# Opening of a four-net modulated-convolution kernel: products on ones, an earlier first tap, scale tables and level steps in another order

## What is computed

```python
def _layer(x, style, w, b, mw, mb, typ):
    s = style @ mw.T + mb
    weight = SCALE * w * s[:, None, :, None]
    demod = lax.rsqrt(jnp.sum(weight * weight, axis=(2, 3)) + EPS)
    weight = weight * demod[:, :, None, None]
    ...
x = x + _L0_attn_ref(_L0_cond_ref(x, cond_512, L0_cond_weights, ...), L0_attn_Wqkv, L0_attn_Wo)
x = x + _L0_ffn_ref(_L0_cond2_ref(x, cond_512, ...), ...)
x = x + _L1_attn_ref(_L1_cond_ref(x, cond_512, ...), ...)
x = x + _L1_ffn_ref(_L1_cond2_ref(x, cond_512, ...), ...)
```

## Time and profile before

| what | value |
|---|---|
| median of 3 runs | 1014.01 us (1013.42 to 1014.83) |
| the profiled execution, its own time | 1012.35 us |
| its span, first to last instruction | 1010.6 us |
| mean granted TensorE clock over the span | 0.987 |
| TensorE busy | 957.1 us, 95% |
| VectorE busy | 556.2 us, 55% |
| GpSimd busy | 469.1 us, 46% |
| ScalarE busy | 232.3 us, 23% |

### The profile page before, as it was taken

The page is one execution under the profiler, slowest core; times in us unless marked ns, Lnnn a source line. Parts: engine busy times, 40 slices in busy tenths (PEclk is TensorE's granted clock), DMA queues, the critical chain, the costliest instruction groups (busy, mean ns, idle before and its releaser), DMA issues.

```text
span 1010.6 us, 15965 instructions
## 1 busy us (share of the span) xinstructions
PE 957.1 (95%) x6766; PEld 712.3 (70%) x6766; DVE 556.2 (55%) x951; ACT 232.3 (23%) x451; POOL 469.1 (46%) x425
## 2 busy tenths in 40 slices
PE   6899999999999999999999879989989999899997
PEld 2337887877887788887888658846857777446953
DVE  7866748567284753848458435243347969302423
ACT  4602122211122212022120210110052666500001
POOL 7934538485575846758376332301322645220300
PEclk9999999999999999999999989989999999999999
DMA  5782101111110111110113075393470000072002
GB/s 137 177 248 67 57 1 43 73 42 53 43 42 32 42 53 42 73 42 2 53 42 111 17 150 152 84 225 55 185 271 1 3 3 3 2 162 67 4 1 83
DMA packets 36287, 74.30 MB, mean 74 GB/s; under 512 B 13492, under 2 KB 22260, under 8 KB 33140
## 3 DMA queue, kind: packets, MB, share of 16 engines
q1 hardware_dynamic: 35880, 72.89, 25.9%
q10 hardware_dynamic: 336, 0.39, 0.1%
HBM read 66.26 MB, written 7.01 MB: 73 GB/s over the span
## 4 chain that ended last, share of the span: by engine, by line
PE 73%; DVE 11%; POOL 6%; ACT 4%; issue 3%; DMA 1%; SPq 0%; POOLq 0%; DVEq 0%; ACTq 0%
PE ps L1208 15%; PE ps L1146 14%; PE ps L1007 8%; PE ps L1462 5%; PE ps L1280 5%; PE ps L1160 4%; POOL w_lo L2354 3%; DVE arena L2010 3%; ACT acts L1507 2%; PE ps L1385 2%; DVE arena L2007 2%; PE ps L1285 1%; DVE h_lo L2019 1%; PE ps L1387 1%; PE ps L1386 1%
## 5 line engine op out<-in xcount | busy, mean ns | idle before, releaser
L2469 POOL TENSOR_TENSOR arena<-arena 128x512 f32<-128x512 f32 x80 | 103.6, 1295 | 122.7 <-DVE arena L2010 122.6
L1146 PE MATMUL ps<-xt_hi,w_hi 128*128 128x512 f32 x320 | 127.8, 399 | 5.5 <-POOL w_lo L2354 2.7
L1146 PE MATMUL ps<-xt_lo,w_hi 128*128 128x512 f32 x320 | 125.5, 392 | 0.0
L1146 PE MATMUL ps<-xt_hi,w_lo 128*128 128x512 f32 x320 | 125.2, 391 | 0.0
L1208 PE MATMUL ps<-h_hi,wo_hi 128*128 128x512 f32 x256 | 104.9, 410 | 11.9 <-DVE h_lo L2019 11.9
L2028 DVE TENSOR_TENSOR fresh<-ps,fresh 128x512 f32<-128x512 f32 x56 | 38.7, 691 | 133.9 <-PE ps L1208 133.8
L2010 DVE TENSOR_TENSOR arena<-ps,rope 64x512 f32<-64x512 f32 x160 | 110.2, 689 | 2.2
L1208 PE MATMUL ps<-h_lo,wo_hi 128*128 128x512 f32 x256 | 103.1, 403 | 0.0
L1208 PE MATMUL ps<-h_hi,wo_lo 128*128 128x512 f32 x256 | 102.4, 400 | 0.0
L2377 POOL TENSOR_TENSOR xt<-arena 128x512 f32<-128x512 f32 x24 | 30.5, 1270 | 136.9 <-DVE arena L1915 136.9
L1600 ACT ACTIVATE h_hi<-ps 128x512 fp32r<-128x512 f32 x64 | 33.1, 603 | 203.1 <-PE ps L1193 203.1
(11 more groups left out here) (325 smaller groups left out, 1882.8 us busy)
## 6 DMA issues: line engine op xcount, KB each, us to landing
acts<-in_w_o_dram SPq DMA_DIRECT2D x8, 1024.0 KB, 5.0
arena<-in_a_wo_dram SPq DMA_DIRECT2D x8, 1024.0 KB, 5.9
arena<-kernel_rows SPq DMA_DIRECT2D x11, 512.0 KB, 11.7
acts<-in_w_qkv_dram SPq DMA_DIRECT2D x3, 1792.0 KB, 7.0
acts<-in_w_qkv_dram SPq DMA_DIRECT2D x4, 1280.0 KB, 6.6
w_l<-kernel_rows SPq DMA_DIRECT2D x10, 512.0 KB, 11.8
arena<-level_rows SPq DMA_DIRECT2D x4, 1024.0 KB, 21.8
stream<-in_x_dram SPq DMA_DIRECT2D x4, 512.0 KB, 6.7
```

The source lines that it names most:

```text
L1146: last = pe.matmul(ps[:, bank, :], w[:, r, cols], x, start=(r == 0 and n == 0), stop=(r == R - 1 and n == 2))
L2469: pool.tensor_tensor(qk[:, chunk, half * HALF:(half + 1) * HALF], rot[:, k % 2, 0, :], rot[:, k % 2, 1, :], ALU.add).then_inc(s_rope, 1)
```

## The change

- TensorE gets 22 products of `ones` with itself (128 columns, into the sixth bank, where no one reads them): 8 ahead of the style products, 4 ahead of net 0's demodulation product, 10 behind it.
- The factors get a semaphore of their own, `s_factor`, and GpSimd's opening waits for that one (and for net 0's taps) alone. `s_setup` counts biases and identity.
- GpSimd makes the zeros of net 0's kernel ahead of net 1's upsampling taps.
- VectorE: `tile_scales` is split. `second_scales` (the tables that need no root) comes earlier, the rest behind the third stage's tiles. The styles of nets 1 to 3, the layer biases and the tap sums come later between the tiles.
- TensorE's level steps, and VectorE's, come later: the first behind net 1's first stage, not in front of it; `turn_levels` behind net 2's first stage.

```diff
-            sp.dma_start(factor[:, :, :], a["factor"]).then_inc(s_setup, 16)
+            sp.dma_start(factor[:, :, :], a["factor"]).then_inc(s_factor, 16)
...
-        N_SETUP = 16 * 3
+        N_SETUP = 16 * 2
...
+            def keep_clock(count):
+
+                for _ in range(count):
+                    pe.matmul(ps[:, COMPOSE - 1, 0:P], ones[:, :], ones[:, :], start=True, stop=True)
+
+            pe.wait_ge(s_const, 1)
+            keep_clock(8)
             pe.wait_ge(s_mod, 48)
...
+            keep_clock(4)
             pe.wait_ge(s_sq, 1)
             demod((0,), 4)
+            keep_clock(10)
...
             kernel_second(1)
+            kernel_first(1)
             level_step(0)
-            kernel_first(1)
+            kernel_third(2)
             level_step(1)
-            kernel_third(2)
+            kernel_second(2)
             level_step(2)
-            kernel_second(2)
+            kernel_first(2)
             turn_levels()
-            kernel_first(2)
             kernel_third(3)
...
+            def second_scales(ns):
+                ch.mark(dve.tensor_copy(in_scale[:, ns, :], s4[:, ns, 0, :]))
+                ch.mark(dve.scalar_tensor_tensor(mid_scale[:, ns, 1, :], s4[:, ns, 1, :], CONV_SCALE, s4[:, ns, 2, :],
+                                                 ALU.mult, ALU.mult))
+                if ns.start:
+                    ch.wait()
+
             def tile_scales(ns):
-                dve.tensor_copy(in_scale[:, ns, :], s4[:, ns, 0, :])
                 for layer in range(2):
                     last = dve.reciprocal(d4[:, ns, layer, :], d4[:, ns, layer, :])
-                dve.scalar_tensor_tensor(mid_scale[:, ns, 1, :], s4[:, ns, 1, :], CONV_SCALE, s4[:, ns, 2, :],
-                                         ALU.mult, ALU.mult)
...
             turn_taps(slice(0, 1))
+            second_scales(slice(0, 1))
             first_scales(slice(0, 1))
+            scaled_tiles(0, range(4))
             tile_scales(slice(0, 1))
             turn_taps(slice(1, 2))
-            scaled_tiles(0, range(4))
+            scaled_tiles(0, range(4, 6))
             styles(slice(1, NET), 7)
-            scaled_tiles(0, range(4, 6))
+            scaled_tiles(0, range(6, 8))
             turn_taps(slice(2, NET))
-            scaled_tiles(0, range(6, 8))
             first_scales(slice(1, NET))
             scaled_tiles(0, range(8, 13))
+            second_scales(slice(1, NET))
+            scaled_tiles(1, range(4))
             tile_scales(slice(1, NET))
-            scaled_tiles(1, range(4))
+            scaled_tiles(1, range(4, 8))
             layer_biases()
+            scaled_tiles(1, range(8, 11))
             tap_sums()
-            scaled_tiles(1, range(4, 8))
+            scaled_tiles(1, range(11, 13))
             level_step(0)
-            scaled_tiles(1, range(8, 13))
+            scaled_tiles(2, range(4))
             level_step(1)
...
-            pool.wait_ge(s_setup, N_SETUP)
+            pool.wait_ge(s_factor, 16)
             first_taps(slice(0, 1))
             upsampled(0, slice(0, 1))
             first_taps(slice(1, NET))
-            upsampled(1, slice(1, 2))
             kernel_zeros(0, 0)
             kernel_zeros(0, 2)
+            upsampled(1, slice(1, 2))
```

5 lines of the change are left out of this document (3 added, 2 removed).

## The result

| | before | changed |
|---|---|---|
| median of 20 runs each, on one chip | 1014.23 us (1012.74 to 1017.21) | **1019.65 us** (1014.42 to 1027.10) |
| ratio to before, 95% interval | | **1.0056** (1.0037 to 1.0074) |
| profiled execution, its span | 1012.35, 1010.6 | 1027.10, 1025.1 |
| mean granted clock of that execution | 0.987 | 0.977 |
| first convolution of the stream begins at | 84.70 | 90.37 |

The change makes the kernel 5.4 us slower; forecast was 1013.6, between 1011.2 and 1015.6.

The account below looks back on a forecast made before the run. The opening's chain of GpSimd taps, ScalarE placements and VectorE's order was taken to hold TensorE. A 2.8 us lead less 1.75 for the clock gave -1.05; between baselines 1012.95 and 1014.7 it took 1013.6 us, range 1011.2 to 1015.6.

Parts of the forecast that it names:

- Part 1: Opening: GpSimd's first taps wait for the factors alone; net 0's upsampling placed 2.2 us earlier, moved kernel zeros cost nothing.
- Part 2: TensorE's 22 products on ones cost nothing, raise the clock; net 0's third stage takes 3.6 us instead of 6.07.
- Part 3 (a): Styles of nets 1 to 3 behind VectorE's tiles: new TensorE wait of 0.7 us from 22.4, lead shrinks to 1.5.
- Part 3 (b) and (c): Net 1's second and first stages start without waits at 32.8 and 38.65; leads 2.7 and 6.9 us.
- Part 3 (d): TensorE's first level step waits for VectorE's tap sums, 44.0 to 47.75; lead 2.8 us, holding all three old waits.
- Part 4: Clock falls behind the new 3.75 us wait before the first level step, costing 1.75 us.
- rival C: Low-clock stretch lasts twice as long and earlier runs lack theirs: +2.45, 1016.5 us; halfway 1015.6. Chance 0.10.
- The sum: Whole change against the profiled execution before: -2.8 + 1.75 = -1.05 us, or 1011.3.
- two baselines: If the runs before have the old low stretch, the change gives 1012.95 us; if they don't, 1014.7.
- A: Clock holds through the level-step wait, or biases run faster and the wait is short: -2.8, 1011.2 us. Chance 0.18.
- D: GpSimd's wait isn't lifted, as net 0's taps land later than the factors: +0.45, 1014.5 us. Chance 0.03.
- B: Products on ones stay at 1.2 GHz; net 0's third stage still takes 6.1 us: +2.85, 1016.9 us. Chance 0.07.

Follow-up runs that it names:

- zeros back: Changed kernel with GpSimd's zeros of net 0's kernel again behind net 1's upsampling taps: 1016.92 us, 1.0027 of before.
- kernels with the level steps at net 2: Changed kernel, zeros behind net 1's upsampling, level steps one stage later still: 1010.93 us. Pair with zeros ahead: 1015.78 with copies as changed, 1011.34 with two-input copies.

## Why the prediction was wrong, by its own steps

- **Part 1** held for the taps: 6.43 (6.3), upsampling at 8.67 (8.65), TensorE's second stage at 16.61 (16.5). Its sentence on the kernel zeros, "It costs nothing, with little to spare", is **the step that failed**. It asked whether GpSimd would be done in time, not who shares something with GpSimd meanwhile. No row of the kernel before showed a copy under a zeroing. What the runs showed in its place: the copies wait for the zeroing, in the change a wait of 3.03 us for TensorE instead of 0.7, and in the median 2.7 us (zeros back) or 4.4 (kernels with the level steps at net 2, twelve runs each).
- **Part 2** had its two times right: the third stage started at 13.04 (12.9) and took 3.73 (3.6). "They cost nothing" was wrong, though: without them it starts at 11.23 and 11.49 (two kernels), since net 0's demodulation comes earlier. So in this execution they take 1.6 to 1.8 us there and give back 2.8 as a shorter stage. What they guard is smaller than the prediction thought: without them the second stage came at 17.6 and 17.9, not 19, and three pairs of kernels differ in the median by 0.4, 0.1 and 0.5 us (ones less no ones), less than their intervals.
- **Part 3 (a)** gave a wait of 0.7 from 22.4; with the zeros back it was 0.66, with them ahead 3.03, because VectorE's "23.0" stood behind the copies. Squared scales 2.4 us late, and everything behind with them.
- **Part 3 (b) and (c)** were right in form, no wait at the second and the first stage of net 1, but at 38.16 and 43.90 instead of 32.8 and 38.65. Of the 5.3 us, 2.35 are the copies, and 3.1 the clock behind the new wait: 1.65 for 0.94 and 5.95 for 3.60. This second stretch had no place in the prediction, which thought a wait of 0.7 harmless; with 3.03 it was not.
- **Part 3 (d)** named the right wait, place and releaser: 4.26 (3.75). With the zeros back it began and ended within 0.8 us of the forecast (44.77 to 48.05 for 44.0 to 47.75). The tap sums were 1.9 us long, not 1.25. GpSimd ran two-input work of 384 and 512 columns beside them, before of 192; that this is the reason was not tested.
- **Part 4** took 1.75 for the low stretch; it lasted 6.8 us and not 3.4 in all three executions of the change, and the prediction had that in rival C. With the zeros back the wait of 3.28 and 3.97 us was followed by 3.4, as taken. Half of 6.8, less the part in which TensorE waited anyway (52.1 to 53.7), is 2.6.
- **The sum** for the profiled opening was -1.05; measured was +5.7 (90.37 against 84.70), 6.7 more: 2.35 for the copies, 3.1 for the clock behind them, 0.6 for the longer tap sums, 0.85 for the longer stretch at the level step, 6.9 together. The sum's two baselines both exist: one execution of before has the low stretch and one doesn't. But the one without it is the longer of the two by 0.9 us, so these two don't bear out that the stretch sets the median of before apart from its first profile.
- **What the collision leaves open.** Without it the forecast would still have been too low: with the zeros back the median is 1016.9, outside the range too. The sum fits that kernel's first profile (first convolution at 83.87 for 84.70 - 1.05 = 83.65), but not its median. The prediction has no price for VectorE's new order itself, and the runs show one: with the level steps where they were, it brings VectorE to its biases 3.0 us later and costs 2.6 us in the median. How much of that stands in the kernel with the zeros back, where the biases come later anyway, is open.
- **The rivals.** C had the longer low stretch right for the change, at 1016.5. That the kernel with the zeros back has 1016.9 is luck, for neither of that kernel's two executions has the long stretch. A and D fell: the clock didn't hold, and GpSimd started at 6.43. B fell in its third stage, 3.73 instead of 6.1. None of the rivals was the collision, so the range ended below the result.
- What the form of the sum hid: the level wait was booked as a harmless end of a gain ("holds all three old waits"). But the gains of (b) and (c) were TensorE's, and the tap sums are VectorE's: VectorE had them done at 42.5 before and at 48.0 with the zeros back. The kernel with the levels at net 2 shows what the same idea gives once VectorE's queue is emptied first.

## What to carry to other kernels

When a step moves in one queue, lay it beside the other engines' work at its new time and look for forms that hold each other up: a small VectorE copy beside a long GpSimd zeroing costs what is left of the zeroing. Another form of the same operation can be the cure, but only where it stands beside a zeroing: with two inputs it was held up by GpSimd's two-input work instead. When a wait is removed on the engine that bounds the kernel, ask which engine's total work comes to its next release; if that isn't moved, the wait comes back, and the clock that falls behind a wait of 3 us can cost as much again (3.1 us behind 3.03 here). Judge by many runs: the one profile of five of the twelve timed here was its fastest run, and that of the change its slowest.

## What was not expected of the hardware

- Two copies of 32x16 numbers took 1.94 to 5.16 us when GpSimd zeroed 128x3072 meanwhile and 0.34 when GpSimd did nothing (kernel with the zeros back), and 0.34 in the two-input form beside the same zeroing.
- Beside GpSimd's two-input first rows it is the other way round: two operations of 32x48 numbers took 0.40 us as copies and 1.94 in the two-input form.
- The clock's rise under products on ones differs from one execution to the next. After the same eight products on ones the same style products took 1.13 us in the kernel with the levels at net 2 and 2.07 in the one with the zeros back, and the next four on ones 1.16 and 2.07:

```profile
5.47 1.13 PE L921 MATMUL ps<-arena 64*128 64x128 f32 x4
```
```profile
5.49 2.07 PE L921 MATMUL ps<-arena 64*128 64x128 f32 x4
```

- Where the clock is up early, net 0's third stage starts early too (10.59 for 12.97), and TensorE then waits 2.23 us for ScalarE's matrices, so nothing is gained; in one execution of the kernel with the zeros back the clock fell behind that very wait (a granted clock of 0.50 from 16.8 to 20.2). Whether this is what cancels the ones' gain in the medians was not tested.
